# Causal attention layers of a four-block transformer: late operand stores move ahead of the first maxima on SyncE, and the exponent table is loaded before ScalarE's wait

## The chip, the cores and the metric

One NeuronCore of a Trainium2 chip runs the whole program. The metric is the device time of one execution in microseconds.

## The reference

Input is x, 2 sequences of 1024 tokens, 128 features. Twelve layers follow each other, each added to the residual x:

- block 0: expert MLP, retention-like attention, expert MLP;
- block 1: x + 0.5·(layer norm, attention, expert MLP), causal attention with rotary embedding, and the first again;
- block 2: ternary MLP, causal attention with rotary embedding, ternary MLP;
- block 3: binary MLP, a selective-decay linear attention, binary MLP.

Four of the twelve layers are softmax attention, and one function builds all four. What it computes, with the causal mask only in two of them:

```
q, k, v = rope(x @ wq), rope(x @ wk), x @ wv      # rope in the causal layers only
s   = scale * q @ k.T        # per head and sequence
s   = where(key <= query, s, -inf)                # causal layers only
out = softmax(s) @ v @ wo
```

## The kernel before

`attention(tag, after, hd, full, rope, scale, double)` at L584 is called for tags f1 and f2 (`full` is true, 32 heads of 4, an expert MLP behind it in the same layer) and for a1 and a2 (`full` is false, causal, 16 heads of 8). In time the order is f1, a1, f2, a2. They are called the full and the causal layers below.

**Units.** Four heads of one sequence are a unit: 16 units in a full layer, 8 in a causal one. For a unit TensorE computes the scores twice. `scores` (L946, with the causal mask added at L952) gives the scores by query row, VectorE takes their row maxima (L1357, `maxima`), and the second product (L1036, in `unit` of `tensor`) gives them transposed with the maxima already subtracted, because the three parts of the maximum sit as three more rows of the operand Qop. ScalarE exponentiates those (L1232), and TensorE multiplies them by the values (L972).

**Operands.** Products are made in bf16 with q and k cut into three bf16 parts each. Tokens come in four chunks of 512 (chunks 0 and 1 are sequence 0, chunks 2 and 3 sequence 1). Per chunk and side (q, k) ScalarE cuts part 0 (L1165) and part 1 (L1171), VectorE takes the remainder (L1381), GpSimd makes part 2 (L1267, `third_part`) and counts it in `cut2`. SyncE then writes the parts to DRAM (`store_cut(ch)`, L820 in causal layers: four DMAs of 96 KB for q and four for k, L825 in full ones) and reads them back in the operands' layout (`load(u, par)`, L724 for q and L729 for k). Sequence 0's first unit has a way of its own (`store_first` and `load_first`, L795, L799, L809).

**Maxima.** TensorE turns a half unit's maxima (L960), ScalarE copies them (L1193 for the first, L1217 later), GpSimd cuts them into three parts (`cut_max`, L1285 to L1289, counted in `mps`), and SyncE writes them to DRAM (L736, 12 KB), waits for that, and reads them back into Qop (L741). Both are in `put_max`.

**Order on SyncE.** SyncE issues every DMA, in program order, all on one hardware queue. In a causal layer the part that matters is, after `store_cut(1)`: wait for sequence 0's stores and for the operand buffer, `load(1, 1)` (operands of unit 1, 576 KB and three times 192 KB), `put_max(0, 0, 0)`, `store_cut(2)`, `store_cut(3)`, then the unit loop.

**Who waits.** TensorE starts unit 0 when the first half's maxima have been placed (`max_placed`), and the score task that belongs to unit 1 waits for `load(1, 1)`; 32 score tasks of unit 0 are done before. ScalarE waits ahead of its unit loop, at `act.wait_ge(s.qst1, N_CUT)` and `act.wait_ge(s.kst1, N_CUT)`, until chunks 2 and 3 have been stored, since the exponents overwrite the tiles they are stored from. TensorE may run three transposed products ahead of the exponents. GpSimd's order in a causal layer is `third_part(2)`, `cut_max(0, 0)`, `third_part(3)`.

**Tables.** ScalarE's functions come from loadable tables. The compiler puts an ACT_TABLE_LOAD directly ahead of the first activation that needs another table; its row has the line of that activation.

**Memory.** `c = Carve()` hands out one large tile, `arena`, in order. Behind `mr` come `ms` (the cut maxima), `rot`, `rem`, and the cut parts of chunks 0 and 1 and of chunk 3's q; chunk 2's parts and chunk 3's k part lie further ahead.

Of the kernel before, what the change touches and what calls it, by code (L numbers as in the profile page):

```python
# [21 lines left out]
ACT = mybir.ActivationFunctionType  # L22
# [60 lines left out]
def macaron(nc, a, out):  # L83
    with ExitStack() as ctx:
        def sb(name, shape, dt=F32):
            return ctx.enter_context(nc.sbuf_tensor(name, shape, dt))[tuple([slice(None)] * len(shape))]
# [28 lines left out]
        ones = sb("ones", [P, P])  # L115
# [468 lines left out]
        def attention(tag, after, hd, full, rope, scale, double):  # L584
# [64 lines left out]
            c = Carve()  # L649
# [14 lines left out]
            mq = c(2 * 16).rearrange("p (n m) -> p n m", n=2)  # L664
            mT = c(P)
            mr = c(P)
            ms = c(2 * 3 * P, BF16).rearrange("p (n a t) -> p n a t", n=2, a=3)

            rot = c((4 if rope else 0) * CHUNK).rearrange("p (m n t) -> p m n t", m=2, n=2) if rope else None
# [48 lines left out]
            def sync(sp):  # L718
# [11 lines left out]
                                         k[u:u + 1, n, :, side * m:(side + 1) * m]  # L730
                                         .to_broadcast([3, hd, m])).then_inc(operands[par], 16)

                def put_max(u, par, qc):

                    sp.wait_ge(s.mps, 2 * u + qc + 1)
                    sp.dma_start(mt[qc].rearrange("i (r t) -> r i t", t=P), ms[0:16, qc, :, :])\  # L736
                        .then_inc(max_stored[qc], 16)
                    sp.wait_ge(max_stored[qc], 16 * (u + 1))
                    for side in range(SIDES):
                        at = P // SIDES * side + MAX_ROW  # L740
                        sp.dma_start(Qop[par][at:at + 3, :, qc * CHUNK:(qc + 1) * CHUNK],  # L741
                                     mt[qc].rearrange("i (j t) -> i j t", j=GROUP)[
                                         :, side * SLOTS:(side + 1) * SLOTS, :])\
                            .then_inc(max_placed[qc], 16)

                def store(u, qc):
                    sp.wait_ge(s.ocp, 2 * u + qc + 1 + 1)
                    for j in range(GROUP):
                        sp.dma_start(ot[(u * GROUP + j) * (hd + 1):(u * GROUP + j + 1) * (hd + 1),
                                        qc * CHUNK:(qc + 1) * CHUNK],  # L750
                                     osb[32 * j:32 * j + hd + 1, qc, :]).then_inc(sums_stored[qc], 16)

                def unit(u, third, par, ahead2, ahead1):
                    if ahead2 and full:
                        sp.wait_ge(s.st, u * 4 * NS + 1)
                        load(u + 2, (par + 2) % 3)
                    put_max(u, par, 1)
                    if ahead2 and not full:

                        sp.wait_ge(s.st, u * 4 * NS + 1)  # L760
                        load(u + 2, (par + 2) % 3)
                    store(u, 0)
                    if not ahead1:
                        sp.wait_ge(s.ost0, 64 * UNITS + 1)
                        load_sums(2)
                    if ahead1:
                        put_max(u + 1, (par + 1) % 3, 0)
                    if ahead1 or double:
                        store(u, 1)
                    if ahead1 and not ahead2:  # L770

                        sp.wait_ge(s.ost0, 64 * (UNITS - 1) + 1)
                        sp.wait_ge(s.ost1, 64 * (UNITS - 1) + 1)
                        load_sums(0)
                        load_sums(1)
                        if not double:
                            load_sums(3, EARLY_ROWS)
# [36 lines left out]
                def store_cut(ch):  # L814
                    b, t0 = ch // 2, (ch % 2) * CHUNK
                    for side, to in ((0, qs), (1, ks)):
                        sp.wait_ge(s.cut2, 2 * ch + side + 1)
                        if HG < 8:
                            for g in range(HG):
                                sp.dma_start(to[b * HG + g, :, :, t0:t0 + CHUNK].rearrange("a r t -> r a t"),  # L820
                                             cut[ch][side][g * rows4:(g + 1) * rows4, :, :])\
                                    .then_inc(cut_stored[b][side], 16)
                        else:
                            for part in range(3):
                                sp.dma_start(to[b * HG:(b + 1) * HG, part, :, t0:t0 + CHUNK],  # L825
                                             cut[ch][side][:, part, :]).then_inc(cut_stored[b][side], 16)
# [8 lines left out]
                if full:  # L835
                    store_cut(0)
                store_cut(1)
                sp.wait_ge(s.qst0, N_CUT)
                sp.wait_ge(s.kst0, N_CUT)
                sp.wait_ge(s.kneg, 2)  # L840
                load(1, 1)
                if full:
                    store_cut(2)
                    store_cut(3)
                    put_max(0, 0, 0)
                else:
                    put_max(0, 0, 0)
                    store_cut(2)
                    store_cut(3)
                sp.wait_ge(s.kneg, 3)  # L850
                if double:
                    sp.dma_start(w1, a["w1_1"]).then_inc(s.we, 16)
# [288 lines left out]
            def scalar(act):  # L1141
# [100 lines left out]
                        copy_out(u, 1)  # L1242


                act.wait_ge(s.qst1, N_CUT)
                act.wait_ge(s.kst1, N_CUT)
                loops(unit)
# [95 lines left out]
            def vector(dve):  # L1343
# [134 lines left out]
                else:  # L1478
# [12 lines left out]
                    projected(3)  # L1491

            return dict(early=table, sync=sync, tensor=tensor, scalar=scalar, gpsimd=gpsimd, vector=vector,
                        sems=s)

# [968 lines left out]
        def boot_vector(dve):  # L2464
# [51 lines left out]
            (retention, ("a0",)),  # L2516
            (moe, ("m1",)),
            (attention, ("f1", 4, True, None, 0.5, True)),
            (attention, ("a1", 8, False, "r1", ROOT8, False)),
            (attention, ("f2", 4, True, None, 0.5, True)),  # L2520
            (ternary_mlp, ("t1",)),
            (attention, ("a2", 8, False, "r2", ROOT8, False)),
# [169 lines left out]
```

## Time and profile before

| | |
|---|---|
| median of 3 runs | 3005.62 us (3000.34 to 3008.44) |
| the profiled execution | 2999.32 us |
| its span, first to last instruction | 2997.6 us |
| mean granted TensorE clock | 0.953 |
| TensorE matmuls busy | 2711.8 us, 90% |
| VectorE busy | 2293.0 us, 76% |
| ScalarE busy | 1830.7 us, 61% |
| GpSimd busy | 530.3 us, 18% |
| moved by DMA | 120.38 MB, 40 GB/s over the span |

Busy shares are means over twelve layers with different limits, so they don't say what the few microseconds around one layer's first unit are worth; that is read from timelines. In a timeline a row is the start, the time from the first to the last of the merged instructions, the engine, the line and the tiles; in brackets the idle time ahead of it and what ended it. SPq rows are the issuing of DMAs, not the transfers. The profiled execution lies 6.3 us (0.2%) below the median of the runs.

### The profile page before, as it was taken

How to read it: one execution, taken by the hardware profiler on the slowest of the kernel's cores; microseconds unless marked ns; L12 is line 12 of the kernel's file. 1: busy time of each engine (PE TensorE's matmuls, PEld its weight loads, DVE VectorE, ACT ScalarE, POOL GpSimd, SP SyncE). 2: the span in 40 equal slices, each digit the busy share in tenths (PEclk: the TensorE clock that was granted, in tenths of full speed). 3: DMA queues.
4: the chain of work that ended last, by engine and by line, in shares of the span. 5: the costliest groups of instructions: out<-in, count | busy, mean ns of one | idle time of the engine just before them, and what ended most of it. 6: DMA issues, size and time to landing. Idle time of an engine off the chain costs nothing. (4 is left out here: it accounts for less than half of the span.)

```text
span 2997.6 us, 44120 instructions
## 1 busy us (share of the span) xinstructions
PE 2711.8 (90%) x16188; PEld 1052.7 (35%) x16188; DVE 2293.0 (76%) x3000; ACT 1830.7 (61%) x3731; POOL 530.3 (18%) x847
## 2 busy tenths in 40 slices
PE   5989898899999999889978999999998889979778
PEld 2437443122222222633332222222226433336336
DVE  5456545999999997667758999999984767765993
ACT  2213323588888888546655888888885656655203
POOL 0000001110111000122312110101001323222771
PEclk9999999799999999989987999999999889989989
DMA  3210121300000000221114000000000221100000
GB/s 116 85 62 2 53 89 56 120 20 20 20 20 20 18 14 25 79 64 47 39 31 138 20 20 16 16 20 20 20 18 21 78 63 39 39 29 29 0 0 16
DMA packets 71968, 120.38 MB, mean 40 GB/s; under 512 B 16905, under 2 KB 44041, under 8 KB 68586
## 3 DMA queue, kind: packets, MB, share of 16 engines
q1 hardware_dynamic: 71754, 117.57, 12.1%
q8 instruction: 129, 2.11, 0.3%
q14 instruction: 85, 0.70, 0.1%
HBM read 94.19 MB, written 23.33 MB: 39 GB/s over the span
## 5 line engine op out<-in xcount | busy, mean ns | idle before, releaser
L1357 DVE TENSOR_REDUCE arena<-ps 128x1 f32<-128x1024 f32 (+7 forms) x1536 | 1566.9, 1063 | 216.9 <-PE ps L952 136.9
L1232 ACT ACTIVATE arena<-ps 128x512 f32<-128x512 f32 (+3 forms) x2816 | 1382.6, 573 | 373.9 <-PE ps L1036 372.9
L946 PE MATMUL ps<-arena 61*128 61x512 bf16 (+4 forms) x2816 | 943.2, 383 | 42.7 <-DVE arena L1357 14.8
L1036 PE MATMUL ps<-arena 64*128 64x512 bf16 (+4 forms) x2816 | 746.8, 372 | 63.6 <-ACT arena L1232 40.4
L972 PE MATMUL ps<-arena 128*32 128x512 f32 (+3 forms) x5632 | 712.9, 578 | 0.4 <-POOL arena L1316 0.3
L1036 PEld LDWEIGHTS ps<-arena 64*128 64x128 bf16 (+1 forms) x2816 | 206.9, 95 | 788.3 <-ACT arena L1232 549.0
L946 PEld LDWEIGHTS ps<-arena 61*128 61x128 bf16 (+1 forms) x2816 | 261.2, 96 | 346.5 <-DVE arena L1357 284.0
L347 PE MATMUL ps<-xnT,moe_up 128*128 128x512 f32 x448 | 216.5, 609 | 0.0
L1285 POOL TENSOR_TENSOR arena<-arena,ones 16x128 bf16<-16x128 f32 x96 | 42.7, 445 | 953.9 <-ACT arena L1217 901.5
L463 ACT ACTIVATE arena<-ps 128x512 f32<-128x512 f32 x112 | 66.5, 597 | 208.0 <-PE ps L347 208.0
L533 DVE TENSOR_TENSOR arena<-arena,ps 128x512 f32<-128x512 f32 x112 | 76.5, 686 | 148.6 <-ACT arena L463 120.7
L972 PEld LDWEIGHTS ps<-arena 128*32 128x32 f32 x5632 | 111.2, 108 | 157.4 <-issue 132.0
L1316 POOL TENSOR_SCALAR_AFFINE_SELECT arena<-arena 128x512 f32<-128x512 f32 x128 | 81.1, 634 | 354.6 <-ACT arena L1232 354.6
L358 PE MATMUL ps<-arena,moe_dn 128*128 128x512 f32 x224 | 116.1, 609 | 17.7 <-DVE arena L542 15.6
L347 PEld LDWEIGHTS ps<-xnT,moe_up 128*128 128x128 f32 x448 | 85.6, 195 | 104.1 <-issue 98.9
L952 PE MATMUL ps<-maskb,identb 128*128 128x128 bf16 x512 | 113.2, 230 | 0.0
L263 POOL TENSOR_SCALAR var<-mv 128x4 f32<-128x4 f32 x40 | 9.6, 239 | 500.9 <-DVE mv L196 500.9
L2181 ACT ACTIVATE xnT<-ps,cols 128x512 f32<-128x512 f32 x8 | 6.2, 778 | 142.8 <-PE ps L278 142.8
L203 DVE TENSOR_SCALAR xn<-x,mv,rstd 128x128 f32<-128x128 f32 x192 | 61.3, 382 | 23.1 <-POOL rstd L264 23.0
L542 DVE TENSOR_TENSOR arena<-arena 128x512 f32<-128x512 f32 x112 | 75.6, 683 | 0.0
L358 PEld LDWEIGHTS ps<-arena,moe_dn 128*128 128x128 f32 x224 | 41.9, 194 | 77.0 <-issue 57.7
L278 PE MATMUL ps<-ident,xn 128*128 128x128 f32 x208 | 34.0, 288 | 37.0 <-DVEq L213 30.6
(241 smaller groups left out, 2504.5 us busy)
## 6 DMA issues: line engine op xcount, KB each, us to landing
arena<-m_w SPq DMA_DIRECT2D x40, 256.0 KB, 3.0
arena<-f_q SPq DMA_DIRECT2D x60, 144.0 KB
arena<-f_k SPq DMA_DIRECT2D x180, 48.0 KB
arena<-in_w SPq DMA_DIRECT2D x4, 2048.0 KB
arena<-a_q SPq DMA_DIRECT2D x14, 576.0 KB
arena<-a_k SPq DMA_DIRECT2D x42, 192.0 KB
a_q<-arena SPq DMA_DIRECT2D x44, 96.0 KB, 2.0
a_k<-arena SPq DMA_DIRECT2D x44, 96.0 KB, 2.0
```

The lines of the kernel that those rows point to most:

```text
L347: nc.tensor.matmul(ps[:, FIRST_UP + tile % RING, :], moe_up[:, w:w + P], xnT[:, ch * CHUNK:(ch + 1) * CHUNK], start=True, stop=True)\
L358: nc.tensor.matmul(ps[:, Y_BANK, :], moe_dn[:, i * D:(i + 1) * D], hid[:, n % HID_RING, :], start=i == 0, stop=i == ALL_HID - 1)\
L463: nc.scalar.activation(sg[:, n % 3, :], ps[:, FIRST_UP + (2 * n) % RING, :], ACT.Silu).then_inc(s.silu, 1)
L533: nc.vector.tensor_tensor(hid[:, n % HID_RING, :], sg[:, n % 3, :], ps[:, FIRST_UP + (2 * n + 1) % RING, :], ALU.mult)\
L542: nc.vector.tensor_tensor(hid[:, n % HID_RING, :], hid[:, n % HID_RING, :], wb[:, min(i, SHARED_AT), :], ALU.mult)\
L946: last = nc.tensor.matmul(at[:, k0 // CHUNK, 0:n], score_rows(Qop[par], j, slice(q0, q0 + P)), score_rows(Kop[par], j, slice(k0, k0 + n)), ...
L952: last = nc.tensor.matmul(at[:, (width - 1) // CHUNK, off:off + P], identb[:, :], maskb[:, 0, :], start=False, stop=True)
L972: last = nc.tensor.matmul(ps[32 * j:32 * j + 32, O_BANK, off:CHUNK], vx[vpar][:, kb, j, :], pr[:, (at % 2) * 4 + j, off:CHUNK], start=kb = ...
L1036: nc.tensor.matmul(ps[:, ring_bank(item), off:CHUNK], shifted_rows(Kop[par], j, slice(kb * P, (kb + 1) * P)), shifted_rows(Qop[par], j, sl ...
L1232: nc.scalar.activation(pr[:, (at % 2) * 4 + j, off:CHUNK], ps[:, ring_bank(item), off:CHUNK], ACT.Exp).then_inc(s.ex, 1)
L1316: nc.gpsimd.affine_select(block, block, [[0, GROUP], [1, P]], ALU.is_ge, zero_fill, base=0, channel_multiplier=-1).then_inc(s.tri, 1)
L1357: nc.vector.tensor_reduce(mq[:, half, j * 4 + qb:j * 4 + qb + 1], src, AXX, ALU.max).then_inc(s.sread, 1)
```

## The change

Three edits, all in `attention`:

1. `put_max` is split into `store_max` and `load_max`. In the causal layers (`not full`) `store_cut(2)` moves ahead of the waits and of `load(1, 1)`, and `store_cut(3)` moves between the store and the load of the first maxima. The full layers keep their order.
2. In all four layers ScalarE computes one exponent of a constant into a new tile `spare`, 128 partitions by 1 word, right ahead of its wait for `qst1`.
3. That tile takes one 4-byte word of `arena` behind `mr`, so everything behind it moves by 4 bytes.

```diff
             mr = c(P)
+            spare = c(1)
             ms = c(2 * 3 * P, BF16).rearrange("p (n a t) -> p n a t", n=2, a=3)
...
-                def put_max(u, par, qc):
-
+                def store_max(u, qc):
                     sp.wait_ge(s.mps, 2 * u + qc + 1)
                     sp.dma_start(mt[qc].rearrange("i (r t) -> r i t", t=P), ms[0:16, qc, :, :])\
                         .then_inc(max_stored[qc], 16)
+
+                def load_max(u, par, qc):
                     sp.wait_ge(max_stored[qc], 16 * (u + 1))
...
+                def put_max(u, par, qc):
+                    store_max(u, qc)
+                    load_max(u, par, qc)
...
                 store_cut(1)
+                if not full:
+                    store_cut(2)
                 sp.wait_ge(s.qst0, N_CUT)
                 sp.wait_ge(s.kst0, N_CUT)
                 sp.wait_ge(s.kneg, 2)
                 load(1, 1)
...
                 else:
-                    put_max(0, 0, 0)
-                    store_cut(2)
+                    store_max(0, 0)
                     store_cut(3)
+                    load_max(0, 0, 0)
...
+                nc.scalar.activation(spare, ones[:, 0:1], ACT.Exp)
                 act.wait_ge(s.qst1, N_CUT)
                 act.wait_ge(s.kst1, N_CUT)
                 loops(unit)
```

## Rows read from the trace of the kernel before

**Rows 1.** Groups by line, ScalarE: count, busy us, mean ns, idle before and its releaser

```profile
L1232 ACT ACT_TABLE_LOAD x3 | 3.8, 1283 | 54.4 <-DMA a_k<-arena 42.2 <-PE ps L1036 12.2
```

**Rows 2.** Timeline of the first causal layer, 1263 to 1302 us: start, duration, engine, line

```profile
1263.94 2.27 POOL L1267 TENSOR_TENSOR arena<-arena 128x512 bf16<-128x512 f32 x2 [5.67 <-ACT arena L1171]
...
1266.69 1.99 SPq L820 DMA_DIRECT2D a_k<-arena  x4
...
1270.62 0.74 SPq L724 DMA_DIRECT2D arena<-a_q  x1
...
1271.40 2.16 SPq L729 DMA_DIRECT2D arena<-a_k  x3
...
1274.64 0.31 SPq L736 DMA_DIRECT2D a_m<-arena  x1
...
1275.91 2.26 POOL L1267 TENSOR_TENSOR arena<-arena 128x512 bf16<-128x512 f32 x2 [1.29 <-ACT arena L1171]
...
1288.48 0.70 SPq L741 DMA_DIRECT2D arena<-a_m  x1
...
1292.11 1.06 PE L1036 MATMUL ps<-arena 128*128 128x512 bf16 x2
...
1294.96 1.87 SPq L820 DMA_DIRECT2D a_k<-arena  x4
...
1298.38 1.28 ACT L1232 ACT_TABLE_LOAD   x1 [21.03 <-DMA a_k<-arena]
1299.68 2.06 ACT L1232 ACTIVATE arena<-ps 128x512 f32<-128x512 f32 x4
...
1301.45 0.72 DVE L1357 TENSOR_REDUCE arena<-ps 128x1 f32<-128x128 f32 x3 [7.67 <-PE ps L952]
```

**Rows 3.** Windows, same layer: busy of PE, PEld, DVE, ACT, POOL; PEclk, DMA share, GB/s

```profile
1268.00:1269.00 1.00, 1.00 (x6) 0.50 (x4) 1.00 (x3) 1.00 (x1) 0.00 (x0) 1.00 1.03 328
...
1276.00:1277.00 1.00, 1.00 (x7) 0.66 (x7) 0.00 (x0) 0.86 (x4) 1.00 (x1) 0.50 0.17 74
...
1288.00:1289.00 1.00, 1.00 (x5) 0.28 (x4) 0.76 (x2) 0.00 (x0) 0.00 (x0) 0.50 0.00 0
```

**Rows 4.** Timeline, same layer, a later load of maxima and the product that waits for it

```profile
1339.06 0.72 SPq L741 DMA_DIRECT2D arena<-a_m  x1
...
1341.49 0.11 PEld L1036 LDWEIGHTS ps<-arena 128*128 128x128 bf16 x2 [0.46 <-DMA arena<-a_m]
```

**Rows 5.** Timeline of SyncE and ScalarE in the second causal layer

```profile
2382.09 2.12 SPq L820 DMA_DIRECT2D a_k<-arena  x4
...
2386.12 0.74 SPq L724 DMA_DIRECT2D arena<-a_q  x1
...
2403.78 0.72 SPq L741 DMA_DIRECT2D arena<-a_m  x1
...
2413.70 1.28 ACT L1232 ACT_TABLE_LOAD   x1 [21.14 <-DMA a_k<-arena]
```

**Rows 6.** Timeline of ScalarE and SyncE, first (544 us on) and second full layer

```profile
544.00 0.27 ACT L1193 ACTIVATE arena<-ps 16x128 f32<-16x128 f32 x1 [16.12 <-PE ps L960]
556.49 1.28 ACT L1232 ACT_TABLE_LOAD   x1 [12.21 <-PE ps L1036]
...
581.81 1.28 SPq L749 DMA_DIRECT2D f_o<-arena  x4
...
1610.86 0.27 ACT L1193 ACTIVATE arena<-ps 16x128 f32<-16x128 f32 x1 [15.70 <-PE ps L960]
1623.36 2.80 ACT L1232 ACTIVATE arena<-ps 128x512 f32<-128x512 f32 x5 [12.23 <-PE ps L1036]
...
1647.68 1.28 SPq L749 DMA_DIRECT2D f_o<-arena  x4
```

**Rows 7.** Timeline of SyncE, first full layer, stores issued right behind its load(1, 1)

```profile
538.66 1.90 SPq L825 DMA_DIRECT2D f_q<-arena  x3
...
544.54 2.62 SPq L825 DMA_DIRECT2D f_k<-arena  x3
```

## The prediction

> **What bounds the kernel now.** The change works on one short stretch in each attention layer: the wait before unit 0. I began with ScalarE's groups by line, to see how often an exponent table is loaded at L1232 and what came before it: three loads of 1.283 us each, two with 42.2 us of idle time ended by the last store of cut operands, one with 12.2 us ended by TensorE [rows 1]. So the two causal layers and the first full layer load it; the second full layer doesn't, because nothing between a1's exponents and f2's replaces the table.
>
> Next I read the timeline of the first causal layer [rows 2]. SyncE has issued the stores of chunk 1 by 1268.68 (1266.69 + 1.99), waits for them to land, and issues load(1, 1) from 1270.62 to 1273.56. The first maxima's 12 KB go out at 1274.64, and SyncE is stuck until 1288.48, 13.84 us. Only then do the stores of chunks 2 and 3 go out, the last at 1296.83 (1294.96 + 1.87). ScalarE, idle for 21.03 us, is released at 1298.38, loads its table, and computes its first exponent at 1299.68. Meanwhile TensorE has had its first products ready since 1292.11, and VectorE stands still for 7.67 us up to 1301.45. No engine is busy in the last stretch: the start of unit 0 is set by SyncE's order alone.
>
> Why 13.84 us for 12 KB? The windows [rows 3] show a DMA share of 0.17 and 74 GB/s while load(1, 1) runs. That is 3 engines of 16 (0.1875). 1152 KB at 74 GB/s are 15.9 us, from about 1272.3 to 1288.2, and at 1288 the rate is 0. The maxima's last shares land as the load ends: they sit behind it on those engines. Everything issued after the load has some share that waits for it.
>
> The second causal layer repeats this [rows 5]: the load goes out at 2386.12, SyncE resumes at 2403.78, the table at 2413.70 after 21.14 us idle, so the first exponent at 2415.00.
>
> **The change part by part. Stores of chunk 2 ahead of the load.** GpSimd finishes chunk 2's third parts at 1266.21 (1263.94 + 2.27) [rows 2], before SyncE gets there, so nothing waits. Eight DMAs are added in front of load(1, 1): at 1.87 to 1.99 us for four [rows 2], 3.9 us, from 1268.68 to 1272.6. The wait for sequence 0's stores, which ended at 1270.62, falls inside them and is free. The load starts 1272.6 − 1270.62 = 2.0 us later and ends 2.0 us later, at 1290.2. Unit 1's scores need it, but TensorE is not through with unit 0's until 1292.11, so this delay is covered; without that cover it would cost up to 2.0 us. SyncE reaches the maxima's store at 1275.5, 0.9 us after they are ready, which costs nothing, since the store is stuck behind the load either way.
>
> **Stores of chunk 3 between store and load of the maxima.** GpSimd makes their third parts from 1275.91 to 1278.17, q then k [rows 2], so SyncE issues q from about 1277.1 and k until 1280.9, and then waits for the maxima's store as before. It resumes at 1288.48 + 2.0 = 1290.5 and issues load_max until 1291.2. Can SyncE run that far ahead of a busy queue? In the first full layer it does: directly behind load(1, 1) it issues twelve DMAs, the first three in 1.90 us, the last three in 2.62 [rows 7], with no stop for the load.
>
> Thirteen engines have their share of chunk 3 done soon after 1281. The three behind the load hold 768/16 = 48 KB each. At 328/16 = 20.5 GB/s for an engine [rows 3] that takes 2.4 us; at 768 KB in 3.8 us, the pace of the late stores before, 3.8. I take 2.4, because the descriptors are already queued. Landing adds 0.5: ScalarE is released at 1290.2 + 2.4 + 0.5 = 1293.1 instead of 1298.38 (bounds 1293 to 1294.5).
>
> The maxima are needed too. A load of maxima on an otherwise free queue releases TensorE 2.43 us after it is issued (1339.06 to 1341.49) [rows 4]: at least 1292.9. If its shares also queue behind chunk 3's, they start at 1292.6, and I add 0.9 for reading and landing. I take 1293.5, since the maxima's store shows that shares do queue [rows 2]. The product takes 0.6, so the first exponent starts at 1294.1: a gain of 1299.68 − 1294.1 = **5.6 us**. Bounds: TensorE can't start before 1292.11, so at most 1299.68 − 1292.7 = 7.0; the low end is 2.8 (below). The second causal layer: 1.9 + 0.1 us later start of the load (2384.21 + 3.9 against 2386.12), SyncE resumes at 2405.8, maxima placed at 2408.8, exponent at 2409.4, against 2415.00: **5.6**.
>
> Here a page of the Trainium skill speaks against the change. "DMA: Bandwidth & Descriptors", section "Why a DMA increments its semaphore by 16 and not by 1", has a copy spread over the largest number up to 16 that divides the slowest dimension on both sides, on the lowest-numbered engines. By that the load of the maxima, three rows long, uses exactly the three engines of load(1, 1). The share of 0.17 agrees for the big load; no row shows it for the small one. By the rule it lands at 1293.5, without it at 1292.9, 0.6 us apart in each causal layer.
>
> **The table.** The constant exponent costs 1.3 us of table and about 0.25 us of work in ScalarE's idle time (12 us in full layers, 21 in causal ones) [rows 1, 6], so nothing. In causal layers its benefit is inside the 5.6 us: the stores release ScalarE at 1293.1, TensorE's product comes at 1294.1, and a table load of 1.3 would only just fit. In the first full layer ScalarE would start 1.28 us earlier, and the second full layer shows what that's worth: without a load the first exponent comes 12.50 us after the first copy of maxima (1610.86 to 1623.36) against 13.78 (544.00 to 556.49 + 1.29), and the first store of results 36.82 us after it against 37.81 [rows 6]. **1.0 us** survives (bounds 0 and 1.3). In the second full layer, 0.
>
> The Trainium skill's "ScalarE: Activation LUTs", section "What ACT_TABLE_LOAD costs", puts about 1.38 us of drain beside the 1283 ns, 2.66 in all. By that the first full layer would gain up to 2.7. In this trace the exponent follows 1.30 us after the load's start [rows 2], and the measurement decides.
>
> **The spare word.** It shifts rot, rem, four of the cut tiles and the cut maxima by 4 bytes. No row here shows an operand off its old place. The nearest are four stores of the same size that take 1.87 or 1.99 us [rows 2], 0.12 apart at the same alignment; I take 0, and for the range up to 1.6 us lost or won over four layers.
>
> Sum: 5.6 + 5.6 + 1.0 = 12.2 us. The profiled execution would be 2999.3 − 12.2 = 2987.1; it lies 6.3 us under the median, so the median goes from 3005.6 to **2993.4**, 0.41% faster. A measurement of this kernel can tell about 0.3%, 9 us, from no change.
>
> **Rivals.** (A) SyncE can't get past the busy queue. Then chunk 3's stores go out from 1290.2 to 1294.0, the load of maxima by 1294.7, placed 2.43 after its start at 1296.4, exponent 1297.0: 2.7 to 2.8 us a layer, total 6.6, 2999.0. For it: these are more descriptors behind a longer load than elsewhere; against it rows 7. Chance 0.11.
>
> (B) The early start is given back. Unit 0 begins at a granted clock of 0.50, as before [rows 3], and what follows may catch on the next load or store. If half of the causal gain goes, 5.6 + 1.0 = 6.6 and again 2999.0. Against it: everything after the start hangs on the start (unit 0's maxima, their store, the next load), and in the full layers 0.99 of 1.28 us survived. Chance 0.16.
>
> (C) Slower. load(1, 1) shares its three engines with chunk 3's stores instead of going first, and unit 1's scores, which TensorE does ahead of unit 0's products, wait for it. It decides only when the load ends later than 1299.1. If the two just interleave, the load ends 2.4 to 3.8 us late, at 1294, and there is still a gain. To lose 9 us in all, each causal layer must start 5 us late, the load ending near 1304: its rate would have to fall from 74 to 40 GB/s. Time 3015. Chance 0.04.
>
> **How the numbers follow.** The forecast has 0.69. Within it a gain under 9 us is possible where the maxima land a microsecond or two late, and A or B can come out above 9, so I leave 0.68 for faster, 0.28 for within 0.3%, and 0.04 for slower. The range goes up to A and B and a little of the runs' spread, 3001, and down to the largest gain, 7.0 + 7.0 + 1.3 = 15.3, or 2990.3, less 4 us for the spread of the median (3000.3 to 3008.4): 2986.
>
> **What would show it.** In causal layers: load(1, 1) issued 2.0 us later; L820 rows ahead of and behind it, the last at about 1281; SyncE resuming 2.0 us later; no table load behind the long wait; VectorE's gap of 7.67 us down to about 2; the first exponent about 5.6 us earlier against the layer's start. The first full layer's first store should come 36.8 us after its first copy of maxima. I am wrong if chunk 3's L820 rows come only after the load ends (A), if the first exponent is early and unit 1 isn't (B), or if TensorE waits for arena<-a_k (C).

## The result, and the profile after

The changed kernel takes 2992.01 us (median of 5, 2987.87 to 2996.38) against 3005.28 us of the kernel before (median of 5): a ratio of 0.9954, 95% interval 0.9937 to 0.9972. The forecast was 2993.4 in 2986 to 3001. The direction, the size and the main mechanism held; several terms inside it were off, each by less than 1 us, and those of the causal layers nearly cancel.

The profiled execution is the slowest of the five, 2996.38 us with a span of 2994.7, only 2.9 us below the profiled one of before. So I don't compare clock times along the span. The retention layer, which the change doesn't touch, shows why. Windows of that layer and the start of the next in either kernel (busy of PE, PEld, DVE, ACT, POOL; PEclk, DMA share, GB/s), before:

```profile
211.00:325.00 114.00, 100.71 (x1304) 81.03 (x1304) 75.15 (x167) 27.38 (x44) 10.11 (x12) 0.90 0.04 14
```

and after:

```profile
211.00:332.00 121.00, 107.81 (x1304) 85.62 (x1303) 75.21 (x167) 27.38 (x44) 10.11 (x12) 0.83 0.04 13
```

The same 1304 matmuls need 7 us more at a granted clock of 0.83 instead of 0.90. What the change does is therefore read inside a layer, from its first store to DRAM (the first L795 row, L801 after). SyncE in the first causal layer of the changed kernel, whose first store is at 1257.83:

```profile
1276.33 1.87 SPq L826 DMA_DIRECT2D a_k<-arena  x4
1278.25 1.88 SPq L826 DMA_DIRECT2D a_q<-arena  x4
1280.17 1.88 SPq L826 DMA_DIRECT2D a_k<-arena  x4
1282.16 0.74 SPq L725 DMA_DIRECT2D arena<-a_q  x1
1282.94 2.16 SPq L730 DMA_DIRECT2D arena<-a_k  x3
1285.15 0.43 SPq L736 DMA_DIRECT2D a_m<-arena  x1
1286.31 1.74 SPq L826 DMA_DIRECT2D a_q<-arena  x4
1288.09 5.25 SPq L826 DMA_DIRECT2D a_k<-arena  x4
1300.05 0.72 SPq L743 DMA_DIRECT2D arena<-a_m  x1
```

This answers to [rows 2]. Chunk 2's stores stand ahead of the load, chunk 3's behind the maxima's store, and SyncE resumes 42.2 us after the layer's first store, 2.2 later than before (1288.48 − 1248.45 = 40.0; 2.0 forecast). The other engines in the same stretch (timeline):

```profile
1286.64 1.28 ACT L1253 ACT_TABLE_LOAD   x1
...
1287.93 0.20 ACT L1253 ACTIVATE arena<-ones 128x1 f32<-128x1 f32 x1
...
1303.07 0.63 PE L1044 MATMUL ps<-arena 128*128 128x512 bf16 x1 [1.64 <-DMA arena<-a_m]
...
1303.45 2.06 ACT L1240 ACTIVATE arena<-ps 128x512 f32<-128x512 f32 x4 [15.31 <-remote]
```

The table is loaded in idle time. The last thing that unit 0 waits for is now the maxima, for 1.64 us (2.71 in the second causal layer); the first exponent comes 45.6 us into the layer instead of 51.2. VectorE's gap, 7.67 us before, is 1.26 (7.37 and 2.33 in the second causal layer):

```profile
1297.87 4.82 DVE L1366 TENSOR_REDUCE arena<-ps 128x1 f32<-128x1024 f32 x4 [0.21 <-PE ps L960]
1303.95 0.29 DVE L1366 TENSOR_REDUCE arena<-ps 128x1 f32<-128x128 f32 x1 [1.26 <-PE ps L960]
```

Landmarks from the timelines of all kernels that ran, each the start of a row less the start of the layer's first store, in us. "Resumes" is the first load of maxima (L741 of the kernel before), "exponent" the first exponent of the scores (L1232), "end" the last store of results (L749). Full 1 is the first full layer. Each row is one profiled execution.

| kernel | causal 1: resumes, exponent, end | causal 2: resumes, exponent, end | full 1: exponent, end |
|---|---|---|---|
| before | 40.0, 51.2, 290.4 | 40.1, 51.3, 290.2 | 47.9, 691.6 |
| before again | 41.7, 52.9, 290.8 | 39.9, 51.1, 289.2 | 48.0, 691.6 |
| changed | 42.2, 45.6, 284.4 | 42.5, 45.8, 283.3 | 46.8, 691.4 |
| changed again | 43.1, 46.4, 284.3 | 42.8, 46.2, 283.5 | 46.2, 690.6 |
| order only | 42.6, 47.3, 286.8 | 42.6, 47.3, 286.7 | 48.0, 691.6 |
| table only | 40.6, 50.6, 289.3 | 41.1, 51.0, 290.4 | 46.2, 690.6 |
| chunk 2 only | 42.9, 48.9, 287.1 | 42.4, 48.6, 287.7 | 46.5, 690.8 |
| no shift | 43.4, 46.8, 285.4 | 42.5, 45.9, 284.2 | 46.7, 691.4 |
| load last | 27.7, 54.5, 293.2 | 27.7, 54.9, 292.8 | 46.7, 691.4 |
| spread, old order | 34.9, 46.8, 286.2 | 35.4, 47.5, 286.3 | 47.5, 690.8 |
| spread, new order | 38.1, 43.3, 280.7 | 38.5, 44.7, 282.4 | 46.6, 691.2 |

Over two executions and two layers the first exponent moves from 51.6 to 46.0, **5.6 us**, as forecast, and the end of the layer from 290.1 to 283.9, **6.3 us**. Twice 6.3 make 12.6 us; the medians differ by 13.3, and the interval of the ratio spans 8.4 to 18.9, so the times alone can't confirm the sum this closely.

The scatter of a landmark comes mostly from when load(1, 1) is issued. Counted from "resumes", the first exponent comes 11.2 us later in all four causal layers of the kernel before and 3.3 to 3.4 later in all four of the changed one: 7.8 us less, of which 2.2 are given back by resuming later (42.7 against 40.4 on average). That leaves the same 5.6 us.

### The profile page after: what moved, and what is told of

Its sections match the earlier page's. It is cut to its first block and busy times, and to the rows that moved or that the text cites. A ratio compares the mean times of both kernels' runs of the same rounds, so it can differ in the third digit from the quotient of the medians.

```text
span 2994.7 us, 44076 instructions
## 1 busy us (share of the span) xinstructions
PE 2706.1 (90%) x16140; PEld 1052.7 (35%) x16188; DVE 2294.0 (77%) x3000; ACT 1831.5 (61%) x3735; POOL 523.4 (17%) x847
## 3 DMA queue, kind: packets, MB, share of 16 engines
q1 hardware_dynamic: 71754, 117.57, 12.4%
## 5 line engine op out<-in xcount | busy, mean ns | idle before, releaser
L1044 PE MATMUL ps<-arena 64*128 64x512 bf16 (+4 forms) x2768 | 735.4, 371 | 62.0 <-ACT arena L1240 26.9
L954 PEld LDWEIGHTS ps<-arena 61*128 61x128 bf16 (+1 forms) x2816 | 260.4, 96 | 349.4 <-DVE arena L1366 286.7
L1294 POOL TENSOR_TENSOR arena<-arena,ones 16x128 bf16<-16x128 f32 x96 | 42.8, 445 | 955.8 <-ACT arena L1225 903.1
L1427 DVE RECIPROCAL hid<-hid 128x512 f32<-128x512 f32 (+1 forms) x14 | 46.9, 3349 | 26.1 <-DMA hid<-a_o 26.0
```

Source lines behind the costliest of these rows:

```text
L954: last = nc.tensor.matmul(at[:, k0 // CHUNK, 0:n], score_rows(Qop[par], j, slice(q0, q0 + P)), score_rows(Kop[par], j, slice(k0, k0 + n)), ...
L1044: nc.tensor.matmul(ps[:, ring_bank(item), off:CHUNK], shifted_rows(Kop[par], j, slice(kb * P, (kb + 1) * P)), shifted_rows(Qop[par], j, sl ...
```

## The experiments

### Scatter of the landmarks

Both kernels were profiled once more, unchanged.

> The kernel before, profiled once more, to see how far its landmarks scatter. Expected: in the causal layers 51.2 to 51.3 us from the first store to the first exponent and 290.2 to 290.4 to the last store of results; in the first full layer 47.5 to 48.0 to the first exponent and 690.8 to 691.6 to the last store, each within 0.8 us. If the last store in the full layer scatters by more than 0.3, the 1.0 us that I gave to the table there can't be told from nothing.

> The changed kernel, profiled once more. Expected: 45.6 to 45.9 us to the first exponent in both causal layers, 283 to 285 to the last store of results; in the first full layer 46.6 and 691.3. My theory has 5.6 us a causal layer repeat within 0.5, and about 0.2 of the table's 1.3 us left at the full layer's last store.

Measured: the causal landmarks repeat within about 1.7 us (one layer of the kernel before had its exponent at 52.9, because even load(1, 1) was issued 1.6 us later there), the full layer's end within 0.8. Both are more than I expected, for the causal exponents of either kernel too. So the causal gain is clear, and a gain under 0.5 us in the full layer isn't.

### Order without the table

Against the changed kernel:

```diff
-            spare = c(1)
...
-                nc.scalar.activation(spare, ones[:, 0:1], ACT.Exp)
```

> Only the order on SyncE is changed; no constant exponent, no spare word. Measured inside a causal layer, from its first store (a_q from arena) to its first exponent: 51.2 and 51.3 us in the kernel before, 45.6 and 45.8 in the changed one. My theory: the order gives most of it, and the table load comes behind the wait for the first product, so 46.9 in both layers (gain 4.3 each), none in the first full layer, 8.6 us in all, ratio 0.997. Rival 'it is the table': with the load back behind the wait most of the gain goes, about 50. Rival 'the table is hidden anyway': 45.6.

Measured: exponents at 47.3 and 47.3, ratio 0.9963 (0.9951 to 0.9975). The order is most of the gain, and the table load comes behind TensorE's first product, as these rows of its timeline show:

```profile
1292.22 0.71 SPq L742 DMA_DIRECT2D arena<-a_m  x1
...
1295.29 0.63 PE L1043 MATMUL ps<-arena 128*128 128x512 bf16 x1 [1.69 <-DMA arena<-a_m]
...
1295.66 1.28 ACT L1239 ACT_TABLE_LOAD   x1 [17.02 <-remote]
```

The load stands behind the wait for that product, not behind the wait for the stores, so its whole 1.3 us is paid: with the new order the early table is worth 47.3 − 46.0 = 1.3 us a layer. To the end of the layer the order alone gains 3.4 us, 6.8 in all, while the timed ratio says 11.1 us (7.5 to 14.7). The timed differences of the split-load kernels below are also 3 to 5 us above their landmarks. What the rest is stays open. In the eleven traces what lies outside the two causal layers takes between 2417.0 and 2427.0 us, 2417.0 and 2419.0 in the kernel before, 2427.0 and 2418.8 in the changed one, so a few microseconds can't be assigned.

### Table without the order

Against the kernel before:

```diff
             mr = c(P)
+            spare = c(1)
...
+                nc.scalar.activation(spare, ones[:, 0:1], ACT.Exp)
                 act.wait_ge(s.qst1, N_CUT)
```

> Only the constant exponent and its word; the order on SyncE is the old one. My theory: one table load of 1.3 us less in each causal layer (first exponent after 50.0 us instead of 51.3), and 0.4 to 1.0 us in the first full layer, 3 to 3.6 us in all, ratio 0.999. Rival 'the exponents were never the start': 0. Rival 'the spare word slows its neighbours': slower than before.

Measured: 50.6 and 51.0, ratio 0.9989 (0.9978 to 1.0). In this execution the loads were issued 0.5 to 0.6 us later than in the kernel before, which hides part of the expected 1.3. Counted from "resumes" the first exponent comes after 10.0 and 9.9 us, against 11.2 in all four layers of the kernel before: 1.2 to 1.3 us, the time of the table load, as expected. So the rival that the exponents were never the start falls. Of this gain 0.3 us is seen at the ends of the layers (289.9 against 290.1), less than their scatter, and whether the rest is kept isn't settled by this run.

### One of the two moves

Chunk 3's stores behind the load of the maxima again, against the changed kernel:

```diff
                     store_max(0, 0)
-                    store_cut(3)
                     load_max(0, 0, 0)
+                    store_cut(3)
```

> The changed kernel, but chunk 3's stores go out behind the load of the maxima again; chunk 2's stay ahead of load(1, 1). My theory: SyncE resumes 42.2 us after the layer's first store as in the changed kernel; then come the maxima's load and 3.8 us of stores, so the stores land at 48.2 and the first exponent starts there, 3.0 us before the kernel before (51.3) and 2.6 behind the changed one. The maxima's load now has nothing queued ahead of it: if in the changed kernel it queues behind chunk 3's stores on its engines (3.02 us from its issue to TensorE), here it takes 2.4; if not, 3.0 here as well.

Measured: 48.9 and 48.6. So of 5.6 us, chunk 2's move with the early table brings 2.9 and chunk 3's 2.7. The second question was whether the maxima queue behind chunk 3. Here nothing is ahead of them, and still:

```profile
1297.85 0.70 SPq L743 DMA_DIRECT2D arena<-a_m  x1
...
1300.74 0.63 PE L1044 MATMUL ps<-arena 128*128 128x512 bf16 x1 [0.74 <-DMA arena<-a_m]
...
1303.91 2.06 ACT L1240 ACTIVATE arena<-ps 128x512 f32<-128x512 f32 x4 [17.11 <-DMA a_k<-arena]
```

To compare with the 2.43 us of [rows 4], which end at a weight load (PEld), the weight loads of the first products are needed, here and in the changed kernel:

```profile
1300.33 0.14 PEld L1044 LDWEIGHTS ps<-arena 128*128 128x128 bf16 x2 [0.92 <-issue]
```

```profile
1302.65 0.14 PEld L1044 LDWEIGHTS ps<-arena 128*128 128x128 bf16 x2 [1.81 <-issue]
```

From the issue of the maxima's load to the weight load it takes 2.48 us here (2.53 in the second layer) and 2.60 in the changed kernel (2.52 to 2.63 over four layers). The queue costs about 0.1 us, not the 0.6 that I gave it. The row of ScalarE shows the exponents waiting for chunk 3's stores again, as in the kernel before.

### The shift by 4 bytes

Against the changed kernel, with everything behind the spare word moved back to where it was:

```diff
-            spare = c(1)
...
+            c.at = ARENA - 1
+            spare = c(1)
```

> The changed kernel with the spare word at the end of the arena, so that nothing is shifted by 4 bytes. My theory: the shift costs nothing; 45.6 and 45.8 us to the first exponent, and SyncE's pace for chunk stores within 0.1 us of the changed kernel. Rival 'shifted tiles cost': the way to the first exponent is shorter by 0.5 us or more.

Measured: 46.8 and 45.9, 2994.76 us in one execution. In both layers the exponent comes 3.4 us after "resumes", as in the changed kernel. Nothing is gained by leaving the neighbours where they were; the spare word is free within the scatter.

### The cover of load(1, 1)

Against the changed kernel, in the causal layers alone, the maxima go first, then both chunks, and the load is issued last:

```diff
-                if not full:
-                    store_cut(2)
                 sp.wait_ge(s.qst0, N_CUT)
                 sp.wait_ge(s.kst0, N_CUT)
                 sp.wait_ge(s.kneg, 2)
-                load(1, 1)
...
                     store_max(0, 0)
-                    store_cut(3)
                     load_max(0, 0, 0)
+                    store_cut(2)
+                    store_cut(3)
+                    load(1, 1)
```

> The changed kernel with load(1, 1) moved behind all of the stores and both maxima transfers. Tests the cover that I counted on: unit 1's scores wait for this load. My theory: SyncE is stuck for about 2 us instead of 14, all stores are out 36 us after the layer's first store, the load ends near 54, and TensorE now waits for arena from a_k: first exponent at 54 to 55, 3 us later than the kernel before. Rival 'the load is not needed at the start': 44.3.

Measured: SyncE resumes after 1.4 us instead of 13.8, everything is stored early, and the layer starts later than before, at 54.5 and 54.9:

```profile
1276.35 0.30 SPq L736 DMA_DIRECT2D a_m<-arena  x1
1277.76 0.73 SPq L743 DMA_DIRECT2D arena<-a_m  x1
...
1286.19 0.72 SPq L725 DMA_DIRECT2D arena<-a_q  x1
...
1304.19 0.63 PE L1044 MATMUL ps<-arena 128*128 128x512 bf16 x1 [11.44 <-DMA arena<-a_k]
```

TensorE is idle for 11.44 us until unit 1's operands are there. This is the mechanism of rival C, made to happen: the load takes 18.0 us from its issue to TensorE. In the changed kernel it is issued at 24.3, and 18.0 us more make about 42.3 (an estimate). TensorE is through with unit 0's scores 43.6 us into that layer (it waits from 1303.07 − 1.64 = 1301.43 on), which leaves a cover of 1.3 us; in the second causal layer it is 0.2 us by the same estimate (24.5 + 18.0 against 42.7). It also shows that of the 13.8 us of the maxima's store 12.4 are time behind the load.

### Splitting the load

If three engines are the cause, the load should be spread. A DMA that repeats its source three times was split into three that don't, for q (24 partitions each) and k (8 partitions each):

```diff
+                        if not full:
+                            for y in range(3):
+                                sp.dma_start(Qop[par][at + 3 * y * hd:at + 3 * (y + 1) * hd],
+                                             q.rearrange("u a d t -> u (a d) t")[u, :, side * m:(side + 1) * m])\
+                                    .then_inc(operands[par], 16)
+                            for n in range(3):
+                                for y in range(3):
+                                    sp.dma_start(Kop[par][at + (3 * n + y) * hd:at + (3 * n + y + 1) * hd],
+                                                 k[u, n, :, side * m:(side + 1) * m]).then_inc(operands[par], 16)
+                            continue
```

First in the kernel before, with its old order and late table:

> The kernel before with its old order and no early table, but the operand loads of the causal layers split into twelve DMAs of 24 and 8 partitions, without the repeated dimension of 3. My theory: the old order was slow only because load(1, 1) ran on 3 engines for 16 us; spread, its data is in about 2 us after its last issue, the DMA share while it runs is 0.5 to 0.75, SyncE resumes after the maxima's store in about 2 us instead of 13.8, and the first exponent waits for TensorE and the table alone: 45.5 us after the first store instead of 51.3, 11 us in all, ratio 0.996. Rival 'the queue, not the three engines': still over 10 us stuck. Rival 'more DMAs clog SyncE': the units in the middle of the layer take over 31.2 us.

Measured: exponents at 46.8 and 47.5, ratio 0.9957 (0.9945 to 0.997): by the timed ratio as much as the whole change, without touching the order, and by the landmarks less: 4.5 us to the first exponent (5.6 in the changed kernel) and 3.9 to the end (6.3). The rival of clogging didn't come true: from the first exponent to the end it takes 239.4 and 238.8 us, against 237.9 to 239.2 in the kernel before. But SyncE was stuck for 6.9 us behind the load (8.6 in the second layer), not 2:

```profile
1279.05 3.00 SPq L731 DMA_DIRECT2D arena<-a_k  x9
1282.10 0.33 SPq L746 DMA_DIRECT2D a_m<-arena  x1
1289.01 0.74 SPq L751 DMA_DIRECT2D arena<-a_m  x1
```

and its windows (same columns as above) say why:

```profile
1281.00:1282.00 1.00, 0.26 (x2) 0.29 (x3) 1.00 (x2) 0.37 (x1) 0.80 (x2) 1.00 0.76 172
...
1285.00:1286.00 1.00, 0.81 (x5) 0.28 (x5) 0.92 (x2) 0.00 (x0) 1.00 (x2) 0.50 0.54 123
1286.00:1287.00 1.00, 1.00 (x4) 0.38 (x5) 0.71 (x2) 0.00 (x0) 0.01 (x1) 0.50 0.49 115
```

The share of 0.76 is about 12 engines, that of 0.5 is 8. But 123 GB/s over 8.6 engines (0.54 · 16) are 14 GB/s for each, and three engines gave 74/3 = 25. So splitting frees the load from three engines, but each of the more engines is slower; why isn't shown. Then in the changed kernel:

> The changed kernel with the same split loads. My theory: nothing but TensorE's and VectorE's own work is left ahead of the first exponent: 44.3 us after the layer's first store (45.6 in the changed kernel), 1.3 us a layer, 15 us below the kernel before, ratio 0.995. Rival 'the maxima are not what it waits for': 45.6 as in the changed kernel.

Measured: 43.3 and 44.7, median 2984.0 us (6 runs), ratio **0.993** (0.9914 to 0.9947) to the kernel before, the fastest of all. TensorE no longer waits for the maxima: they are loaded at 38.1, and the exponents begin when TensorE and VectorE are through with unit 0's scores, as its first product shows:

```profile
1293.25 0.63 PE L1054 MATMUL ps<-arena 128*128 128x512 bf16 x1 [0.22 <-issue]
```

## Why the prediction was right, point by point

**The stretch.** Right: the start of unit 0 was set by SyncE's order, and the load on three engines was what held it. The new order alone brings the first exponent forward by 4.3 us, splitting the load alone by 4.5, and issuing the load last puts it back by 3.1. "By SyncE's order alone" goes a little too far: it needed the load on three engines as well.

**Chunk 2 ahead of the load.** Right: the load is issued 2.2 us later (2.0), and SyncE resumes 2.2 later. For unit 1's scores this is covered, though the cover is thin, as the load-last kernel shows. For the maxima, which stand behind the load, it is not: the sum rightly has them 2.0 us later, and TensorE now waits 1.6 to 2.7 us for them.

**Chunk 3 between store and load.** The sum was right, three parts of it were not. I had SyncE run ahead of the busy queue without a stop. It doesn't quite: the last four DMAs take 5.25 us in the changed kernel (5.19 in the second layer) instead of 1.9, a single one up to 2.10 us. SyncE stands until 1293.3 and then goes on, over 6 us before it resumes at 1300.05; so rival A exists but lets go in time. The wait of the maxima behind chunk 3's shares, 0.6 us, is about 0.1. And from the weight load to the first exponent it takes 0.8 us (1302.65 to 1303.45), not the 0.6 that I gave the product. From SyncE's resuming to the first exponent I had 3.6 us (1290.5 to 1294.1); it is 3.4, and the resuming is 0.2 later than forecast. That the result is 5.6 to the tenth is luck, since the landmarks of one kernel scatter by up to 1.7 us. The rule of the Trainium skill ("DMA: Bandwidth & Descriptors", "Why a DMA increments its semaphore by 16 and not by 1") on how many engines a copy uses agrees with the shares in the split kernels (24 rows: 0.76 of 16 engines, about 12; 8 rows: 0.5); the 0.6 us by which, as I read it, the maxima would land later are not borne out.

**The table.** In the causal layers 1.3 us, inside the 5.6. I had said that a table load would only just fit between the release by the stores and the first product. The order-only kernel shows that it doesn't fit at all, since it stands behind the wait for the product. In the first full layer the step that failed is "1.0 us survives". The exponent does come 1.3 us earlier there (47.9 over four executions without the early table, 46.5 over seven with it), but the layer ends at 691.4 against 691.1, within the scatter. ScalarE is the least busy of the three engines there: from 570 to 1200 us of the kernel before TensorE is busy for 615.6 of 630 us, VectorE for 582.7 and ScalarE for 538.0. VectorE's idle time at the start hardly changes. Before:

```profile
557.58 1.22 DVE L1357 TENSOR_REDUCE arena<-ps 128x1 f32<-128x1024 f32 x1 [0.42 <-PE ps L946]
559.11 3.72 DVE L1357 TENSOR_REDUCE arena<-ps 128x1 f32<-128x1024 f32 x3 [0.31 <-PE ps L946]
564.62 4.62 DVE L1357 TENSOR_REDUCE arena<-ps 128x1 f32<-128x1024 f32 x4 [1.79 <-PE ps L946]
```

After:

```profile
567.20 2.36 DVE L1366 TENSOR_REDUCE arena<-ps 128x1 f32<-128x1024 f32 x2 [0.42 <-PE ps L954]
569.98 2.35 DVE L1366 TENSOR_REDUCE arena<-ps 128x1 f32<-128x1024 f32 x2 [0.42 <-PE ps L954]
573.94 4.62 DVE L1366 TENSOR_REDUCE arena<-ps 128x1 f32<-128x1024 f32 x4 [1.60 <-PE ps L954]
```

2.52 us of waits before, 2.44 after, each for TensorE's scores: the earlier exponents don't shorten them. Whether TensorE or VectorE bounds the layer wasn't tested. I had taken the difference between the two full layers of one execution for the table's effect; the second full layer ends anywhere from 690.2 to 691.6 us after its first store, though no kernel needs a table load there.

**After the start.** Rival B had some of the gain given back. In the changed kernel none is: 0.7 us more by the end of the layer. In the order-only kernel 0.9 of 4.3 us is given back. Both are below the scatter of the ends (289.2 to 290.8 in the kernel before), but one thing goes with them, the moment at which TensorE is granted the full clock. Windows of the second causal layer, whose first exponent is at 2415.00 before:

```profile
2418.00:2420.00 2.00, 2.00 (x14) 1.11 (x15) 1.31 (x4) 1.26 (x4) 1.76 (x5) 0.50 0.00 0
2420.00:2422.00 2.00, 2.00 (x13) 0.41 (x5) 0.20 (x1) 0.29 (x2) 0.29 (x1) 0.70 0.03 6
```

and at 2411.02 after:

```profile
2412.00:2414.00 2.00, 2.00 (x13) 1.27 (x12) 0.73 (x4) 1.65 (x6) 0.85 (x2) 0.59 0.04 12
2414.00:2416.00 2.00, 2.00 (x18) 0.82 (x18) 1.50 (x4) 1.18 (x4) 1.76 (x5) 1.00 0.00 0
```

PEclk rises from 0.50 (1.2 GHz) to 1.00 (2.4 GHz) 5 to 7 us behind the first exponent before and 1 to 3 us behind it after. In the first causal layers of the same two traces the difference is smaller. From the mean clock of the stretch from 1 us ahead of each first exponent to 15 us behind it I work out 3.5 to 6.4 us for the four layers of the kernel before, 2.2 to 4.1 for the changed one and 5.7 and 6.7 for the order-only one. Over the 22 causal layers of all traces it is 1.9 to 7.0 us, and what follows the first exponent takes 237.3 to 239.5 us; the two go together (correlation 0.91, some 0.4 us for each microsecond of delay). What sets the moment stays open. The length of TensorE's gap before the start doesn't decide it: the order-only kernel waits for the maxima as briefly as the changed one (1.69 and 2.04 us) and is granted the full clock on average 1.3 us later than the kernel before, whose TensorE waits 6.2 us for the first exponents in the second layer.

**The table's price.** The first exponent, of the constant or of the scores, follows the load's start by 1.29 to 1.30 us in all traces, so the 2.66 us of the Trainium skill's "ScalarE: Activation LUTs", "What ACT_TABLE_LOAD costs", are not seen here.

## What to carry to other kernels

The DMA that takes 13.8 us for 12 KB here isn't slow, it stands behind another: look at the DMA share while it waits, and if that is a few sixteenths, a transfer ahead of it uses a few engines and splitting it is worth trying, not only moving it. Stores that somebody waits for go ahead of a long load whose own user is later, up to the microsecond at which that user is ready; whatever stands behind the load is delayed with it. An engine that starts earlier brought nothing where two others were busier.

## What the runs showed of the hardware that I had not expected

- SyncE can be held by a queue it has filled: one 96 KB issue took 2.10 us instead of 0.44, with load(1, 1), the maxima's store and seven stores of chunk 3 issued just ahead of it. With the load split (last kernel above) the same four issues took 1.88 us instead of 5.25.
- Reading the same operand rows over 8 to 12 engines gave each 12 to 14 GB/s, over 3 engines 25 GB/s. The windows of the split load from 1279 to 1288 us add up to 1.16 MB, nearly all of its 1.18, so on some three times the engines it took about 9 us instead of 16.
- The granted clock in an untouched layer differed between two executions (0.90 and 0.83), worth 7 us: more than half of the whole effect studied here. The first full layer's first store came 509.8 to 519.4 us into the eleven executions, in no order by kernel.
